# Softmax stage of a four-layer block: in a wide score tile, head 1's products follow head 0's two products behind

## Chip, cores and metric

The kernel runs on one core of a Trainium2 chip. The metric is the device time of one execution in microseconds (us); lower is better. Of the kernel before, three runs are shown, and their median is what a change is measured against.

## What is computed

The reference is a chain of six residual sublayers over x of shape (4, 1024, 128): two top-4-of-32 expert layers around a linear attention, then two top-2-of-8 expert layers around a 16-head softmax attention. Only that attention matters here:

```python
Q = einsum('bmd,hdk->bhmk', x, P_q)          # 16 heads, width 64
K = einsum('bmd,hdk->bhmk', x, P_k)
V = einsum('bmd,hdv->bhmv', x, P_v)
logits = einsum('bhmk,bhnk->bhmn', Q, K) * 8
logits = where(causal, logits, -inf)
w = softmax(logits, axis=-1)                 # 1024 x 1024 per batch and head
o = einsum('bhmm,bhmv->bhmv', w, V)          # the diagonal of w alone
y = einsum('bhmv,hdv->bmd', o, P_o)
```

Since `o` takes the same index twice, only the diagonal of the softmax is needed. For each query that is its own exponential over the sum of the exponentials of its row, so every score has to be formed and summed, but no product of weights and V follows.

## The kernel before, in words

The kernel is written engine by engine: each of its eleven stages gives TensorE, ScalarE, VectorE, GpSimd and SyncE their own list of instructions in a fixed order, and semaphores tie them together. The softmax stage is `softmax_diagonal`. It has 32 units (`UNITS`), one per pair of heads and batch: 8 pairs (`PAIRS`) for each of 4 batches. A head is 64 wide, so the two heads of a pair lie in partitions 0 to 63 and 64 to 127 (`head`), and a score product of one head uses 64 of the 128 rows of the array.

Per unit TensorE does the following (`tensor`, L2858 to L2870):

- It projects queries and keys of the next unit: four banks of three products of 128x512 (`project`, L2807 to L2809). ScalarE copies two of the banks out (L2877) and VectorE the other two (L2883). GpSimd then splits queries and keys into a high and a low part (`split`, L2747 to L2761), since each score is the sum of three products: high x low, low x high, high x high (`passes`).
- It forms the scores of the eight query blocks q of 128 queries. Block q has (q + 1) x 128 keys, its causal part. The order is `ORDER` = 1, 5, 6, 4, 2, 3, 7, and block 0 goes with block 2. Blocks 4 to 7 are wide tiles: `big` (L2819 to L2831) puts each head into two PSUM banks of half the keys each. The others go to `little` (L2841 to L2856), with one bank per head. After tile 1 come the products that give the pair's own scores, eight rows in the trace (`diagonals`, L2837).

In the text "tile 5" is the scores of query block 5, 768 wide, and likewise tiles 6 (896), 4 (640) and 7 (1024). A product of tile 5 has 384 columns, of tiles 6, 4 and 7 448, 320 and 512.

For each tile and head VectorE adds the mask and finds the lowest score, in one custom reduction over the whole tile (L2954, followed by a short read-out row of the accumulator), and ScalarE forms the exponentials in place with that value as bias and sums them (L2934, also followed by a reading of the accumulator). With ScalarE's reading the semaphore `exp_done` rises and the banks are free. Both go through the tiles in the same order, head 0 before head 1.

The eight PSUM banks are given out round robin: a unit takes 4 for the projections and 22 for its tiles, and what takes a bank waits for whoever used it last, eight places before (`wait_bank`, L2724). For the wide tiles that comes to:

- tile 5: head 0 takes the banks of head 1 of the previous unit's tile 7; head 1 takes two projection banks, copied out by VectorE
- tile 6: head 0 takes two projection banks, copied out by ScalarE; head 1 the two banks of tile 1
- tile 4: head 0 takes the banks of tile 5's head 0, head 1 those of tile 5's head 1
- tile 7: head 0 takes the banks of tile 4's head 0, head 1 those of tile 4's head 1

At a batch's end VectorE has some extra work with the sums (`invert`, `divide`, `keep`, `arguments`).

Of the kernel before, what the change touches and what calls it, by code (L numbers as in the profile page):

```python
# [24 lines left out]
P = 128  # L25
# [77 lines left out]
def build(nc, I, out):  # L103
# [9 lines left out]
    def sem(name):  # L113
        if free:
            return free.pop()
        held.append(nc.alloc_semaphore(name))
        return held[-1]
# [58 lines left out]
    def bank(k):  # L176
        return psum[:, k, :]
# [2478 lines left out]
    def softmax_diagonal(split, used):  # L2656
# [5 lines left out]
        S = {n: sem(f"a1_{n}") for n in names}  # L2662
# [14 lines left out]
        ORDER = (1, 5, 6, 4, 2, 3, 7)  # L2677
        LITTLE = {1: (1,), 2: (2, 0), 3: (3,)}
        DIAG, QUARTERS = 1, 4
        NS = 2 * len(ORDER)  # L2680
        BANKS_OF = [4 if q >= BT else 2 for q in ORDER]
        PER_UNIT = NP + sum(BANKS_OF)
# [8 lines left out]
        def first_bank(u, n):  # L2691
            at = before_unit(u) + (NP if u < UNITS - 1 else 0) + sum(BANKS_OF[:n])
            return at % BANKS

        def scored_before(u, n, a):
            return u * NS + 2 * n + a

        def wide(q):
            return (q + 1) * P

        def big_scores(u, n, a):
            k = first_bank(u, n) + 2 * a
            return psum[:, k % BANKS:k % BANKS + 2, 0:wide(ORDER[n]) // 2]

        def small_scores(u, n, q, a):
            at = 3 * P if q == 0 else 0
            return psum[:, (first_bank(u, n) + a) % BANKS, at:at + wide(q)]
# [5 lines left out]
        def spare_of(u, a):  # L2713
            return psum[:, (first_bank(u, ORDER.index(DIAG)) + a) % BANKS, 2 * P:]

        def which(u):
            return u % PAIRS, u // PAIRS

        def turned_own(src):
            return src.rearrange("p (k c e) -> p c k e", k=2, c=QUARTERS)[:, :, :, 0:H1]  # L2720
# [3 lines left out]
        def wait_bank(pe, k, freed, count):  # L2724

            if k in last_user:
                pe.wait_ge(*last_user[k])
            last_user[k] = (S[freed], count)
# [18 lines left out]
        def gpsimd(pool):  # L2747
            def split(v):
                s = v % 2
                wait_out(pool, v, "k")  # L2750
                if v >= 2:
                    pool.wait_ge(S["scored"], (v - 1) * NS)
                pool.tensor_copy(KH[s], KF[s]).then_inc(S["k_hi"], 1)
# [38 lines left out]
        def turn_own(pe, b, dst):  # L2792
            pe.wait_ge(S["diag_in"], (b + 1) * PAIRS)
            for k in range(2):
                last = pe.transpose(dst[:, k * P:(k + 1) * P], own[:, b % 2, k * P:(k + 1) * P], ident[:])
            return last

        def project(pe, v, k):
            kind, half = PROJECT[k]
            g, b = which(v)  # L2800
            wh, wl = (all_w[:, 2 * (kind == "k") + w, g * P:(g + 1) * P] for w in range(2))
            at = slice(b * SEQ + half * BLK, b * SEQ + (half + 1) * BLK)
            to = project_bank(v, k)
            if k == 0 and v < 2:
                pe.wait_ge(split["xl_done"], 2 if v == 0 else 4)
            wait_bank(pe, to, "out_dve" if half else "out_act", out_count(v, kind, half))
            pe.matmul(bank(to), wh, xl[:, at], start=True, stop=False)  # L2807
            pe.matmul(bank(to), wl, xh[:, at], start=False, stop=False)  # L2808
            pe.matmul(bank(to), wh, xh[:, at], start=False, stop=True).then_inc(S["projected"], 1)  # L2809

        def tensor(pe):
            def passes(u):
                s = u % 2
                return ((QH[s], KL[s]), (QL[s], KH[s]), (QH[s], KH[s]))

            def head(w, a, at, n):
                return w[a * DK:(a + 1) * DK, at:at + n]

            def big(u, n):  # L2819
                q = ORDER[n]  # L2820
                half = wide(q) // 2
                for a in range(2):
                    for k in range(2):
                        wait_bank(pe, (first_bank(u, n) + 2 * a + k) % BANKS, "exp_done", scored_before(u, n, a) + 1)
                for p, (qs, ks) in enumerate(passes(u)):
                    for k in range(2):
                        for a in range(2):
                            last = pe.matmul(big_scores(u, n, a)[:, k, :], head(qs, a, q * P, P),  # L2828
                                             head(ks, a, k * half, half), start=(p == 0), stop=(p == 2))
                            if p == 2 and k == 1:  # L2830
                                last.then_inc(S["scored"], 1)  # L2831

            def diagonals(u):
                g, b = which(u)
                pe.wait_ge(S["multiplied"], u + 1)
                for c in range(QUARTERS):
                    last = pe.matmul(spare_of(u, 1)[32 * c:32 * (c + 1), :], pair_ones[:, H1 - 2 * g:3 * H1 - 2 * g],  # L2837
                                     prod[:, c * 2 * P:(c + 1) * 2 * P], start=True, stop=True)
                last.then_inc(S["scored"], 1)

            def little(u, n):  # L2841
                for a in range(2):
                    wait_bank(pe, (first_bank(u, n) + a) % BANKS, "exp_done", scored_before(u, n, a) + 1)
                for q in LITTLE[ORDER[n]]:
                    for p, (qs, ks) in enumerate(passes(u)):
                        for a in range(2):
                            last = pe.matmul(small_scores(u, n, q, a), head(qs, a, q * P, P), head(ks, a, 0, wide(q)),
                                             start=(p == 0), stop=(p == 2))
                            if p == 2 and q == LITTLE[ORDER[n]][-1] and q != DIAG:
                                last.then_inc(S["scored"], 1)  # L2850
                if ORDER[n] == DIAG:
                    g, b = which(u)
                    if g == 0 and b > 0:
                        last = turn_own(pe, b - 1, spare_of(u, 0))
                    last.then_inc(S["scored"], 1)
                    diagonals(u)  # L2856

            for u in range(UNITS):  # L2858
                if 0 < u < UNITS - 1:
                    for k in range(NP):  # L2860
                        project(pe, u + 1, k)
                if u == 0:
                    pe.wait_ge(split["xl_done"], NB)
                pe.wait_ge(S["k_lo"], u + 1)
                pe.wait_ge(S["q_lo"], u + 1)
                for n, q in enumerate(ORDER):
                    if q >= BT:
                        big(u, n)
                    else:
                        little(u, n)  # L2870
            pe.wait_ge(S["exp_done"], UNITS * NS - 2)

# [12 lines left out]
        def batch_of(w, b):  # L2885
            return w[:, b * QT:(b + 1) * QT, :]
# [5 lines left out]
        def invert(dve, b):  # L2892
            dve.wait_ge(S["exp_done"], (b + 1) * PAIRS * NS)
            dve.reciprocal(batch_of(esum, b), batch_of(esum, b)).then_inc(S["inverted"], 1)
# [10 lines left out]
        def arguments(dve, b, src):  # L2905
            all_t = batch_of(arg, b).rearrange("p (c k) e -> p c k e", k=2)
            dve.wait_ge(S["exp_done"], (b + 1) * PAIRS * NS)
            dve.tensor_tensor(all_t, all_t, turned_own(src), ALU.subtract).then_inc(S["arg_set"], 1)
# [3 lines left out]
        def end_pe(pe, j):  # L2912
            if j == 0:
                pe.wait_ge(S["exp_done"], UNITS * NS)
                turn_own(pe, PER - 1, bank(B_OWN)).then_inc(S["own_turned"], 1)
# [85 lines left out]
    def program():  # L3001
# [17 lines left out]
        E2 = dict(E, y_sent=[sem(f"m1e_y_sent{a}") for a in range(2)])  # L3019
        experts_of = moe_experts(E, sort.S)  # L3020
        softmax, unit_first, closing = softmax_diagonal(split, used)
        combine = moe_combine(experts_of.S, split, unit_first)
        sort_2 = sorted_ffn(sort_sems("a1o", False), dn=o_dn, relu=False, ahead=softmax.S, closing=closing, **heads)
# [103 lines left out]
```

## Time and profile before

| | |
|---|---|
| three runs | 1712.15, 1709.97, 1704.38 us |
| median | 1709.97 us |
| profiled execution, from its first to its last instruction | 1712.5 us (the page gives no other time for it) |
| TensorE busy with products | 1436.3 us, 84% of the span |
| VectorE busy | 1339.1 us, 78% |
| ScalarE busy | 1030.1 us, 60% |
| GpSimd busy | 861.2 us, 50% |
| mean granted TensorE clock | 0.938 of full |
| the softmax stage's reductions, L2954 | 512, first at 885.5 us, last at 1353.4 |

All times in the rows are in us from the start of the profiled execution, unless marked ns. PE is TensorE's products, PEld its weight loads, DVE VectorE, ACT ScalarE. A time order gives start, duration, engine, line, operation, and in square brackets how long the engine had been idle before and what ended that. Of instructions that are merged into one row, xN gives their number, and the duration runs from the first one's start to the last one's end.

### The profile page before, as it was taken

Reading aid. Unit: us, or ns where it says so; the run is one execution under the profiler, and the core shown is the slowest. Engines: PE = TensorE matmul, PEld = TensorE weight load, DVE = VectorE, ACT = ScalarE, POOL = GpSimd, SP = SyncE. Lnnn points to the kernel's source line nnn. Section 1 sums busy time; section 2 is a strip of 40 time slices with the busy share of each in tenths; the row PEclk is TensorE's granted clock in tenths of the full one; section 3 lists DMA queues with packets and bytes.
Section 4 is the critical chain, followed back from the end, with each engine's and each line's share of the span. In section 5 each row is a group of like instructions: output and inputs, shape, how many; then the busy total and the mean of one; then the engine's idle time right before and its main releaser. Section 6 shows DMA issues by size and latency. Waiting matters only on the chain.

```text
span 1712.5 us, 30382 instructions
## 1 busy us (share of the span) xinstructions
PE 1436.3 (84%) x8651; PEld 1046.6 (61%) x8653; DVE 1339.1 (78%) x3816; ACT 1030.1 (60%) x2170; POOL 861.2 (50%) x743
## 2 busy tenths in 40 slices
PE   5999999898999995999368878878888799769990
PEld 4778877655666653777245656655656566457770
DVE  7599998566666666787679999999999667857876
ACT  7444442374232316888469988989989622258880
POOL 5756643210133342676656665656656225637663
PEclk9999998999999996999779999999999899879995
DMA  9993010000011104222399900000000001122225
GB/s 189 166 165 44 1 26 26 2 1 13 19 32 42 32 22 98 66 71 66 86 180 166 127 1 1 1 1 1 1 1 1 1 13 35 42 55 68 67 62 148
DMA packets 182172, 91.69 MB, mean 54 GB/s; under 512 B 43829, under 2 KB 176902, under 8 KB 182048
## 3 DMA queue, kind: packets, MB, share of 16 engines
q1 hardware_dynamic: 167840, 71.19, 24.5%
q0 software_dynamic: 9984, 16.89, 3.1%
q10 hardware_dynamic: 4224, 2.10, 0.4%
q8 instruction: 61, 1.00, 0.3%
q14 instruction: 63, 0.52, 0.1%
HBM read 32.59 MB, written 61.18 MB: 55 GB/s over the span
## 4 chain that ended last, share of the span: by engine, by line
PE 63%; DVE 13%; ACT 10%; issue 6%; DMA 4%; POOL 3%; SPq 1%; DVEq 0%; POOLq 0%; ACTq 0%
PE psum L1362 9%; PE psum L2828 7%; ACT psum L2934 7%; PE psum L658 5%; PE psum L659 4%; PE psum L660 4%; DVE psum L2954 4%; PE psum L2807 2%; PE psum L2264 2%; PE psum L2266 2%; PE psum L2265 2%; PE psum L2276 2%; PE psum L2808 2%; PE psum L2809 2%; PE psum L2278 2%
## 5 line engine op out<-in xcount | busy, mean ns | idle before, releaser
L2934 ACT ACTIVATE psum<-psum,gate 128x128 f32<-128x128 f32 (+7 forms) x512 | 366.7, 719 | 51.2 <-DVE gate L2954 44.3
L2954 DVE CUSTOM_DVE_ANT_0 psum<-psum,cmask 128x128 f32<-128x128 f32 (+7 forms) x512 | 375.0, 785 | 28.2 <-PE psum L2828 26.6
L2440 POOL DMA_INDIRECT answers<-ed,answer_to x184 | 201.4, 1094 | 78.7 <-issue 50.2
L1362 PE MATMUL psum<-raw_all,w 128*128 128x512 f32 x384 | 196.3, 594 | 1.5 <-DVE raw_all L1490 1.5
L658 PE MATMUL psum<-xl,wreg 128*128 128x512 f32 x320 | 181.8, 568 | 2.5 <-ACT psum L2934 1.3
L1488 DVE SCALAR_TENSOR_TENSOR raw_all<-psum,hg 128x512 f32<-128x512 f32 x128 | 88.1, 690 | 65.9 <-PE psum L660 64.5
L2828 PE MATMUL psum<-spare_sets_room 64*128 64x384 f32 (+3 forms) x768 | 95.0, 380 | 46.3 <-ACT psum L2934 46.2
L2828 PE MATMUL psum<-hh,hl 64*128 64x384 f32 (+3 forms) x768 | 93.3, 376 | 41.6 <-ACT psum L2934 41.5
L659 PE MATMUL psum<-xh,wreg 128*128 128x512 f32 x320 | 126.6, 396 | 0.0
L660 PE MATMUL psum<-xh,wreg 128*128 128x512 f32 x320 | 126.3, 395 | 0.0
L2828 PEld LDWEIGHTS psum<-spare_sets_room 64*128 64x128 f32 x768 | 71.8, 195 | 71.0 <-ACT psum L2934 59.1
L2356 DVE TENSOR_TENSOR hl<-gate,hh 128x512 fp32r<-128x512 f32 x92 | 63.3, 688 | 63.1 <-ACT hh L2318 32.2
L2828 PEld LDWEIGHTS psum<-hh,hl 64*128 64x128 f32 x768 | 71.0, 194 | 66.7 <-ACT psum L2934 52.4
L1235 POOL TENSOR_TENSOR hl<-hg,hh 128x512 fp32r<-128x512 f32 x65 | 85.8, 1323 | 47.5 <-ACT hh L1167 46.4
L2934 ACT ACTIVATION_READ_ACCUMULATOR psum<-psum,gate 128x1 f32 x512 | 105.1, 205 | 0.0
L819 POOL DMA_INDIRECT rows<-raw_all,row_no x64 | 61.7, 965 | 78.5 <-PE psum L660 63.9
L819 POOL DMA_INDIRECT rows<-row,row_no x64 | 61.9, 966 | 69.1 <-PE psum L660 52.1
L1167 ACT ACTIVATE hh<-hg 128x512 fp32r<-128x512 f32 x86 | 54.1, 632 | 67.1 <-DVE hg L1198 65.2
L201 POOL TENSOR_TENSOR spare_p<-spare_p 128x1 f32<-128x1 f32 x63 | 20.5, 326 | 142.7 <-DVE row_no L780 69.2
L658 PEld LDWEIGHTS psum<-xl,wreg 128*128 128x128 f32 x320 | 61.0, 191 | 39.2 <-issue 27.9
L1362 PEld LDWEIGHTS psum<-raw_all,w 128*128 128x128 f32 x384 | 72.2, 189 | 20.3 <-DVE raw_all L1490 2.3
L2264 PE MATMUL psum<-xl,xh 128*128 128x512 f32 x184 | 81.6, 443 | 0.0
(431 smaller groups left out, 4053.0 us busy)
## 6 DMA issues: line engine op xcount, KB each, us to landing
rows<-blank SPq DMA_DIRECT2D x146, 258.0 KB, 8.3
row<-rows SPq DMA_DIRECT2D x46, 256.0 KB
raw_all<-answers SPq DMA_DIRECT2D x32, 256.0 KB, 4.2
w<-in_L_ffn_W_dram SPq DMA_DIRECT2D x16, 256.0 KB, 3.1
answers<-ed,answer_to POOLq DMA_INDIRECT x184
x<-in_L_attn_x_dram SPq DMA_DIRECT2D x4, 512.0 KB, 6.6
out_dram<-x ACTq DMA_DIRECT2D x8, 256.0 KB, 4.3
rawD<-in_L_ffn_values_dram SPq DMA_DIRECT2D x4, 256.0 KB, 6.5
```

What stands on the lines that cost most here:

```text
L658: pe.matmul(dst, wh, xl[:, blk(i)], start=start, stop=False)
L659: pe.matmul(dst, wl, xh[:, blk(i)], start=False, stop=False)
L660: return pe.matmul(dst, wh, xh[:, blk(i)], start=False, stop=stop)
L819: pool.indirect_dma_start(rows, bass.IndirectOffsetOnAxis(ap=row_no[:, i % 2, c, t:t + 1], axis=0), row_of(i)[:, t, c, :], None).then_inc( ...
L1235: pool.tensor_tensor(hl[:, j % SLOTS, :], kept[n % len(kept)], hh[:, j % SLOTS, :].bitcast(F32), ALU.subtract).then_inc(S["lo_pool"], 1)
L1362: pe.matmul(bank(B_OUT[i % 2]), col(dn, j), hidden[:, n % HID, :], start=(j == 0), stop=(j == nf - 1)).then_inc(S["dn_done"], 1)
L1488: last = dve.scalar_tensor_tensor(out, raw, 0.0, gates_now, ALU.max, ALU.mult)
L2264: pe.matmul(dst, high, xb[:, b.odd, 1], start=True, stop=False)
L2440: pool.indirect_dma_start(answers, bass.IndirectOffsetOnAxis(ap=answer_to[:, out.odd, t:t + 1], axis=0), y_row[:, out.odd, t, :], None, bo ...
L2828: last = pe.matmul(big_scores(u, n, a)[:, k, :], head(qs, a, q * P, P), head(ks, a, k * half, half), start=(p == 0), stop=(p == 2))
L2934: return act.activation(src, src, ACT.Exp, bias=kept_at(arg, u, q, a), scale=-1.0, accum_out=kept_at(esum, u, q, a))
L2954: return dve.tensor_tensor_reduce(src, src, mask, 1.0, 3e38, ALU.add, ALU.min, kept_at(arg, u, q, a))
```

## The change

`big` alone changes. Before, all four bank waits of a wide tile (two banks for each of two heads) stood ahead of its first product, and the twelve products alternated: head 0, head 1, head 0, head 1. Now head 0's six products are counted m = 0 to 5, a bank's wait stands directly ahead of the first product that writes it, and head 1's product m is written after head 0's product m + 2 (`SKEW = 2`). Every product's operands and its bank, the semaphores and the counts waited for are those of before. Head 0's scores are still signalled before head 1's.

```diff
         DIAG, QUARTERS = 1, 4
+        SKEW = 2
...
             def big(u, n):
                 q = ORDER[n]
                 half = wide(q) // 2
-                for a in range(2):
-                    for k in range(2):
+                steps = [(p, k) for p in range(3) for k in range(2)]
+
+                def step(a, m):
+                    p, k = steps[m]
+                    qs, ks = passes(u)[p]
+                    if p == 0:
                         wait_bank(pe, (first_bank(u, n) + 2 * a + k) % BANKS, "exp_done", scored_before(u, n, a) + 1)
-                for p, (qs, ks) in enumerate(passes(u)):
-                    for k in range(2):
-                        for a in range(2):
-                            last = pe.matmul(big_scores(u, n, a)[:, k, :], head(qs, a, q * P, P),
-                                             head(ks, a, k * half, half), start=(p == 0), stop=(p == 2))
-                            if p == 2 and k == 1:
-                                last.then_inc(S["scored"], 1)
+                    last = pe.matmul(big_scores(u, n, a)[:, k, :], head(qs, a, q * P, P),
+                                     head(ks, a, k * half, half), start=(p == 0), stop=(p == 2))
+                    if m == len(steps) - 1:
+                        last.then_inc(S["scored"], 1)
+
+                for m in range(len(steps) + SKEW):
+                    if m < len(steps):
+                        step(0, m)
+                    if m >= SKEW:
+                        step(1, m - SKEW)
```

How TensorE's instructions move is seen in the second unit, tiles 5, 6 and 4. A row is one or several equal matmuls. Semaphores carry the names of their first users: `f0_oT_ready` is `exp_done`, `a0_kv_done` is `out_dve` (VectorE's copies) and `a0_f_done` is `out_act` (ScalarE's copies). Before, on TensorE:

```order
L2828 MATMUL psum<-spare_sets_room 128x384 [waits a0_kv_done,f0_oT_ready]
L2828 MATMUL psum<-spare_sets_room 128x384 x11
L2828 MATMUL psum<-spare_sets_room 128x448 [waits f0_oT_ready,a0_f_done]
L2828 MATMUL psum<-spare_sets_room 128x448 x11
L2828 MATMUL psum<-spare_sets_room 128x320 [waits f0_oT_ready]
L2828 MATMUL psum<-spare_sets_room 128x320 x11
```

And after the change, on TensorE in the same place:

```order
L2830 MATMUL psum<-spare_sets_room 128x384 [waits f0_oT_ready] x2
L2830 MATMUL psum<-spare_sets_room 128x384
L2830 MATMUL psum<-spare_sets_room 128x384 [waits a0_kv_done]
L2830 MATMUL psum<-spare_sets_room 128x384
L2830 MATMUL psum<-spare_sets_room 128x384 [waits a0_kv_done]
L2830 MATMUL psum<-spare_sets_room 128x384 x6
L2830 MATMUL psum<-spare_sets_room 128x320 [waits f0_oT_ready] x2
L2830 MATMUL psum<-spare_sets_room 128x320
L2830 MATMUL psum<-spare_sets_room 128x320 [waits f0_oT_ready]
L2830 MATMUL psum<-spare_sets_room 128x320
L2830 MATMUL psum<-spare_sets_room 128x320 [waits f0_oT_ready]
L2830 MATMUL psum<-spare_sets_room 128x320 x6
```

(Tile 6's rows stand between the two.) The single wait ahead of a tile has become four: two ahead of head 0's first two products, then, behind head 0's third and fourth product, one each ahead of head 1's first two. The other engines have the same instructions in the same order as before.

## Rows read from the trace of the kernel before

**Rows 1.** The page's slices: busy tenths in 40 slices of 42.8 us.

```profile
DVE  7599998566666666787679999999999667857876
ACT  7444442374232316888469988989989622258880
```

**Rows 2.** Busy times by stretch, three of 32 units: PE, PEld, DVE, ACT, POOL, PE clock, DMA.

```profile
943.96:958.90 14.94, 12.71 (x96) 9.93 (x99) 13.45 (x36) 13.17 (x36) 9.11 (x5) 0.89 1.28 171
...
1017.33:1034.45 17.12, 12.99 (x96) 9.42 (x99) 15.66 (x38) 13.30 (x37) 9.08 (x5) 0.90 0.01 1
...
1092.07:1106.26 14.19, 11.57 (x96) 8.48 (x95) 13.46 (x36) 13.15 (x36) 9.13 (x5) 1.00 0.00 1
```

**Rows 3.** Time order of VectorE in the clean unit from 1092.07.

```profile
1093.85 0.97 DVE L2954 CUSTOM_DVE_ANT_0 psum<-psum,cmask 128x768 f32<-128x768 f32 x1 [0.39 <-PE psum L2828]
...
1095.65 0.14 DVE L2954 DVE_READ_ACCUMULATOR2_ANT gate<- 128x1 f32 x1
1095.77 1.10 DVE L2954 CUSTOM_DVE_ANT_0 psum<-psum,cmask 128x896 f32<-128x896 f32 x1
...
1097.84 0.14 DVE L2954 DVE_READ_ACCUMULATOR2_ANT gate<- 128x1 f32 x1
1098.22 0.83 DVE L2954 CUSTOM_DVE_ANT_0 psum<-psum,cmask 128x640 f32<-128x640 f32 x1 [0.24 <-PE psum L2828]
...
1102.57 0.14 DVE L2954 DVE_READ_ACCUMULATOR2_ANT gate<- 128x1 f32 x1
1102.73 1.23 DVE L2954 CUSTOM_DVE_ANT_0 psum<-psum,cmask 128x1024 f32<-128x1024 f32 x1
```

**Rows 4.** Time order of TensorE's products in the same unit.

```profile
1091.38 0.62 PE L2847 MATMUL psum<-hh,hl 64*128 64x256 f32 x6
...
1092.50 1.31 PE L2828 MATMUL psum<-hh,hl 64*128 64x384 f32 x12
1094.28 1.48 PE L2828 MATMUL psum<-hh,hl 64*128 64x448 f32 x12 [0.46 <-ACT psum L2934]
1097.07 1.15 PE L2828 MATMUL psum<-hh,hl 64*128 64x320 f32 x12 [1.31 <-ACT psum L2934]
...
1101.06 1.66 PE L2828 MATMUL psum<-hh,hl 64*128 64x512 f32 x12 [0.85 <-ACT psum L2934]
1102.66 0.50 PE L2807 MATMUL psum<-xl,wreg 128*128 128x512 f32 x1
```

**Rows 5.** Time order of ScalarE in the same unit: tiles 5, 6 and 4.

```profile
1095.71 0.19 ACT L2934 ACTIVATION_READ_ACCUMULATOR psum<-psum,gate 128x1 f32 x1
1095.83 0.88 ACT L2934 ACTIVATE psum<-psum,gate 128x768 f32<-128x768 f32 x1
1096.62 0.19 ACT L2934 ACTIVATION_READ_ACCUMULATOR psum<-psum,gate 128x1 f32 x1
1096.96 0.98 ACT L2934 ACTIVATE psum<-psum,gate 128x896 f32<-128x896 f32 x1
...
1098.91 0.19 ACT L2934 ACTIVATION_READ_ACCUMULATOR psum<-psum,gate 128x1 f32 x1
1099.14 0.77 ACT L2934 ACTIVATE psum<-psum,gate 128x640 f32<-128x640 f32 x1
...
1100.62 0.19 ACT L2934 ACTIVATION_READ_ACCUMULATOR psum<-psum,gate 128x1 f32 x1
```

**Rows 6.** The same order of TensorE, cut off inside tile 5 (stretch 1092.3 to 1092.79).

```profile
1092.50 0.61 PE L2828 MATMUL psum<-hh,hl 64*128 64x384 f32 x4
```

**Rows 7.** Time order of TensorE, start of the projections: product, then next load.

```profile
1088.45 0.50 PE L2807 MATMUL psum<-xl,wreg 128*128 128x512 f32 x1
...
1088.56 0.19 PEld L2808 LDWEIGHTS psum<-xh,wreg 128*128 128x128 f32 x1
```

**Rows 8.** Time order of ScalarE and TensorE after the stage's last exponential.

```profile
1355.79 0.19 ACT L2934 ACTIVATION_READ_ACCUMULATOR psum<-psum,gate 128x1 f32 x1
1356.04 0.69 PE L2795 MATMUL psum<-ident,own 128*128 128x128 f32 x2 [1.50 <-ACT psum L2934]
```

## The prediction

> **What bounds the kernel now.** The slices of the page come first [rows 1]: from the twenty-first slice on, for eleven slices, VectorE and ScalarE are both near nine tenths busy. That is the softmax stage, some 472 of the 1712.5 us, and the only place that the edit touches. Next I cut the stage at the start of each unit (the first score tile of a head pair on VectorE) and asked for the busy times of the 32 stretches [rows 2]. Eighteen units take 14.19 to 14.33 us at full TensorE clock (the row from 1092.07 is one), three take 14.89 to 14.96 with the granted clock at 0.89 (the row from 943.96), eight stand round the ends of batches, where VectorE has extra work (the row from 1017.33 is the longest but one), and the first one and the last two are ramps (15.81, 13.18 and 16.38). In the clean unit TensorE is busy for 11.57, VectorE 13.46, ScalarE 13.15 of 14.19 us: none is full, so a ring of waits sets the length, and the time order shows it.
>
> On VectorE [rows 3] a read-out row normally begins together with the next reduction. Where the reduction is later, VectorE waited: 0.12 us before tile 6 (1095.65 to 1095.77), 0.38 before tile 4 (1097.84 to 1098.22), 0.16 before tile 7 (1102.57 to 1102.73). Tile 5 shows 0.39 as well. TensorE [rows 4] in turn stands 0.46, 1.31 and 0.85 us before tiles 6, 4 and 7, each time for ScalarE's exponentials, which free the banks.
>
> The ring that sets the unit, from one start of tile 5 on VectorE (1093.85) to the next [rows 3 to 5]: ScalarE ends tile 4, head 1, at 1100.62 + 0.19 = 1100.81, so 6.96 us later; TensorE begins tile 7 0.25 after that (1101.06); its six slots last 1.60 until the projections (1102.66); from the first projection to tile 1 it is 2.93 (1088.45 to 1091.38) [rows 4, 7]; and from there to tile 5 on VectorE 2.47 (1091.38 to 1093.85). The sum is 14.21.
>
> **What the change costs and gives.** No instruction is added or removed apart from semaphore waits; 48 products a unit change places, in 32 units.
>
> Slots: two products of different heads start together. The first two pairs of tile 5 take 0.61 us, all six 1.31 [rows 4, 6], so a pair costs (1.31 - 0.61) / 4 = 0.175. In the new order the twelve products need eight slots, if nothing makes head 1 wait: two of head 0 alone, four pairs, two of head 1 alone. A lone product I price as a pair, 0.175, because the nearest row, a product over all 128 rows, also has the next load beside it [rows 7]; it could be no cheaper, and dearer by a whole load, 0.19, which is a rival below. So TensorE may be held 0.35 us longer per tile of this size. In tiles 5 and 6 this lies beside VectorE: head 1 is ready two slots, 0.35, after head 0, and VectorE is busy with head 0 for 0.9. Where head 1's banks come late, in tiles 4 and 7, three products of head 0 run before the wait, and after it six slots remain as before, so nothing is added there; what stands behind that wait are head 0's last three products, and they are released with head 1's first.
>
> The wait itself gets shorter. Today the four bank waits precede the first product, the release at 1096.62 + 0.19 = 1096.81 is followed by the product at 1097.07: 0.26 [rows 4, 5], and 0.25 for tile 7. In the new order head 1's first product has one wait of its own. For one wait the nearest row is the transpose at 1356.04, 0.06 after the release at 1355.79 + 0.19 [rows 8]. I take that and save 0.19; the bounds are 0 and 0.20.
>
> VectorE's waits: tile 6 can start beside tile 5's last product instead of at 1094.28, since its head 0 only needs ScalarE's two copies; tile 5 begins at 1092.50, and with two slots more it has ended by 1092.50 + 1.31 + 0.35 = 1094.16, at least 0.12 before today's start of tile 6, and its last product may run beside tile 6's first: the 0.12 goes. Tile 4, head 0, has three slots of 0.14 fewer behind the release and 0.19 less latency: 0.61 earlier, against a wait of 0.38 and the 0.12 by which VectorE now arrives earlier, so that goes too. Tile 7's 0.16 goes the same way. VectorE alone would then need 14.19 - 0.66 = 13.53 us a unit. Tile 5's own wait stays, since its head 0 follows head 1 of the previous tile 7 and then tile 1's products.
>
> ScalarE is late next. It stood idle 0.22 before tile 6 (a reading starts at 1095.71 and the next exponential at 1095.83, so after the reading at 1096.62 it could be 1096.74; it was 1096.96) and 0.11 before tile 4 (1098.91, so 1099.03, against 1099.14) [rows 5]. Of this some 0.10 remains, since tile 6 still reaches it a little late. It ends tile 4 head 1 about 0.20 earlier than now. The ring becomes (6.96 - 0.20) + (0.25 - 0.19) + 1.60 + 2.93 + 2.47 = **13.82 us**, longer than VectorE's 13.53, so this ring decides and the gain is 0.38 per unit.
>
> Clock: the rows at 0.89 cost 14.94 - 14.21 = 0.73 us each [rows 2]. What TensorE did before the clock fell was to stand still: the longest hole of a clean unit is the 1.31 before tile 4 [rows 4]. Head 0 now fills that hole with three early products, and two lone slots lengthen the tile before it. I expect the three stretches in clean units and two of those beside batch ends to go: 3 x 0.73 + 1.0 = 3.2 us.
>
> Sum: 21 units x 0.38 = 8.0; the eight round batch ends, where VectorE's extra work hides most of it, 8 x 0.2 = 1.6; ramps 0.6; clock 3.2. **13.4 us**. The profiled execution spans 1712.5, which would become 1699.1; that span lies 2.5 above the median of the three runs, 1709.97, from which I forecast 1696.6.
>
> One rule speaks against the edit. The load rows show the next load starting 0.11 after the first projection starts, while that product, over the same rows of the array, runs for another 0.39 [rows 7]. The Trainium skill, page "TensorE: Matmul & The Clock Gate", Part 3, says that a load overlaps running products only when they use another row group. By that rule the projections could not run as they do, so the trace differs from it. Were it true of the lone products, the forecast would be the second rival's.
>
> **Rivals.**
> 1. Larger gain, 0.06: the ring is cut further and VectorE's 13.53 decides. 21 x 0.66 + 5.4 gives about 19 us: 1690.7.
> 2. A lone product also pays for its load, 0.05. Head 0 of tile 5 starts with two of them, in the ring: 2 x 0.19 = 0.38, which takes back the whole 0.38. The clock's 3.2 remains: about 1707. For it: no lone half-array product exists in this trace. Against: the projections.
> 3. The waits moved are not those that end last, 0.13. In tiles 5 and 6 little hangs on banks anyway; if only the shorter latency of tile 7 counts, 21 x 0.19 = 4.0 and half of the clock's: 1704.
> 4. Slower, 0.05: products two steps apart no longer share the array. A tile then takes twelve slots instead of six; tile 5's 1.31 is five slots and 0.43 of start and end, and with the same 0.43 the slots of tiles 6, 4 and 7 come to 0.21, 0.14 and 0.25 [rows 4], so TensorE gets 6 x 0.775 = 4.6 us more a unit. It has 14.19 - 11.57 = 2.6 free [rows 2], the point from which this decides; 2.0 over in 31 units is 62 us: about 1772. Against it: both orders put the two heads side by side in the instruction stream, on other rows and other banks.
> 5. The low clock comes in every unit, 0.03: it is in ten of the 32 units now; 22 more x 0.73 = 16, less the 10.2 otherwise gained: 1716.
>
> **How the numbers follow.** The forecast has 0.68. Its own range is 1690 to 1702: latency saved or not in the ring (21 x 0.19 = 4) and the clock's part absent or complete (3). Half a per cent, 8.5 us, is about what a measurement of this kernel can tell from no change; that line is at 1701.4. Faster: forecast and larger gain, 0.74. Same: the second, third and fifth rival, 0.21. Slower: the fourth, 0.05. The range 1688 to 1706 leaves out the slow cases, the second rival and some noise; the three runs of before alone span 7.8 us.
>
> **What would show it.** Clean units of 13.8 instead of 14.2 us; VectorE's waits before tiles 6, 4 and 7 below 0.05 and the one before tile 5 unchanged; TensorE's tile 4 split, three lone products, a pause, then pairs; the first product after the pause 0.06 behind ScalarE's reading; fewer units with the clock at 0.89. It is wrong if lone products start over 0.25 apart in tile 5, if pairs no longer start together, or if the unit stays at 14.2 with VectorE's waits gone, which would mean that another ring had been as long.

## The result and the profile after

The changed kernel runs in 1691.89 us (median of 4 runs, 1691.54 to 1692.65) against 1708.81 for the kernel before (median of 4, 1704.38 to 1712.15). The recorded ratio is 0.9911, 95% interval 0.9896 to 0.9927 (the two medians alone give 0.9901): faster by 0.9%. The forecast was 1696.6 within 1688 to 1706. One execution in the whole study stands apart, one of ten of e2 with 2832.72 us; it is left out of every comparison, and its cause is not known.

The span of the profiled execution went from 1712.5 to 1690.5 us, 22.0 less. Not all of that is the change's: the softmax stage, from VectorE's first reduction to ScalarE's last reading, went from 470.5 to 453.6 us, 16.9 less. The stage also began 1.1 us earlier and what follows it was 4.0 us shorter, in parts of the program that the edit does not touch. Over all profiles of this study the stage began anywhere from 879.1 to 885.5 us, so differences of a few us are read below from the stage and its units, not from the total.

The page's slices of the changed kernel (busy tenths in 40 slices), TensorE, VectorE and ScalarE:

```profile
PE   5999999898999994999549999999989899769990
...
DVE  7599998567667675787679999999989767857876
ACT  7444432364223234888569999989989622268880
```

Busy times by stretch in the changed kernel (columns as in [rows 2]): a clean unit, a unit with a low clock, and the longest unit.

```profile
1095.15:1108.92 13.77, 12.90 (x93) 9.56 (x92) 13.25 (x35) 12.87 (x36) 9.11 (x5) 1.00 0.01 2
```

```profile
1167.06:1181.52 14.46, 13.61 (x96) 10.85 (x98) 13.42 (x36) 13.05 (x35) 9.14 (x5) 0.88 0.00 1
1237.89:1256.49 18.60, 16.34 (x96) 11.58 (x92) 15.72 (x39) 14.45 (x38) 10.11 (x6) 0.82 0.01 2
```

The clean unit takes 13.77 us where [rows 2] had 14.19. TensorE's busy time went up, from 11.57 to 12.90, though it does the same products: the three early products of a split tile count as busy time alone.

Time order of VectorE in that unit (the reductions of tiles 5, 6, 4 and 7, head 0, with the reading before them), to be held against [rows 3]:

```profile
1096.95 0.97 DVE L2962 CUSTOM_DVE_ANT_0 psum<-psum,cmask 128x768 f32<-128x768 f32 x1 [0.39 <-PE psum L2830]
...
1098.75 0.14 DVE L2962 DVE_READ_ACCUMULATOR2_ANT gate<- 128x1 f32 x1
1098.75 1.13 DVE L2962 CUSTOM_DVE_ANT_0 psum<-psum,cmask 128x896 f32<-128x896 f32 x1
...
1100.85 0.15 DVE L2962 DVE_READ_ACCUMULATOR2_ANT gate<- 128x1 f32 x1
1100.85 0.87 DVE L2962 CUSTOM_DVE_ANT_0 psum<-psum,cmask 128x640 f32<-128x640 f32 x1
...
1105.24 0.14 DVE L2962 DVE_READ_ACCUMULATOR2_ANT gate<- 128x1 f32 x1
1105.24 1.27 DVE L2962 CUSTOM_DVE_ANT_0 psum<-psum,cmask 128x1024 f32<-128x1024 f32 x1
```

Each reduction starts with the reading before it: the waits of 0.12, 0.38 and 0.16 us are gone, and tile 5's 0.39 is unchanged. A new wait of 0.11 stands before tile 1, which starts 0.71 us after the copy before it where 0.60 is usual.

Time order of TensorE in the same unit, against [rows 4], and ScalarE's reading that frees tile 5, head 1:

```profile
1094.49 0.62 PE L2855 MATMUL psum<-spare_sets_room 64*128 64x256 f32 x6
...
1095.61 2.90 PE L2830 MATMUL psum<-spare_sets_room 64*128 64x384 f32 x24
1099.06 0.70 PE L2830 MATMUL psum<-spare_sets_room 64*128 64x320 f32 x3 [0.55 <-ACT psum L2942]
1099.97 1.15 PE L2830 MATMUL psum<-spare_sets_room 64*128 64x320 f32 x9 [0.22 <-ACT psum L2942]
...
1103.04 2.34 PE L2830 MATMUL psum<-spare_sets_room 64*128 64x512 f32 x12
1105.31 0.50 PE L2808 MATMUL psum<-xl,wreg 128*128 128x512 f32 x1
```

```profile
1099.73 0.19 ACT L2942 ACTIVATION_READ_ACCUMULATOR psum<-psum,gate 128x1 f32 x1
```

Tile 4 shows the change as written: three products of head 0, a pause, then nine. The first of the nine starts at 1099.97, 0.05 after the reading ended (1099.73 + 0.19 = 1099.92); before, it was 0.26 [rows 4, 5]. Tile 5 and tile 6 are merged into one row of 24, with no pause.

### The profile page after: what moved, and what is told of

It is laid out like the page before. It is cut to its first block, busy times and chain, and to the rows that moved or that the text cites. A ratio compares the mean times of both kernels' runs of the same rounds, so it can differ in the third digit from the quotient of the medians.

```text
span 1690.5 us, 30128 instructions
## 1 busy us (share of the span) xinstructions
PE 1469.8 (87%) x8653; PEld 1074.6 (64%) x8653; DVE 1335.7 (79%) x3816; ACT 1022.8 (61%) x2170; POOL 861.6 (51%) x743
## 4 chain that ended last, share of the span: by engine, by line
PE 63%; DVE 14%; ACT 8%; issue 6%; DMA 3%; POOL 3%; DVEq 2%; SPq 1%; POOLq 0%; ACTq 0%
PE psum L1362 9%; PE psum L2830 7%; PE psum L658 5%; PE psum L2855 5%; PE psum L659 4%; PE psum L660 4%; ACT psum L2942 4%; DVE psum L2962 3%; PE psum L2808 2%; PE psum L2809 2%; PE psum L2810 2%; PE psum L1121 1%; PE psum L190 1%; PE psum L1123 1%; PE psum L1122 1%
## 5 line engine op out<-in xcount | busy, mean ns | idle before, releaser
L2830 PE MATMUL psum<-spare_sets_room 64*128 64x384 f32 (+3 forms) x768 | 115.3, 369 | 16.2 <-ACT psum L2942 16.2
L2830 PE MATMUL psum<-hh,hl 64*128 64x384 f32 (+3 forms) x768 | 113.1, 376 | 13.4 <-ACT psum L2942 13.4
L2830 PEld LDWEIGHTS psum<-spare_sets_room 64*128 64x128 f32 x768 | 85.9, 185 | 45.3 <-ACT psum L2942 39.3
L2830 PEld LDWEIGHTS psum<-hh,hl 64*128 64x128 f32 x768 | 87.9, 194 | 39.0 <-ACT psum L2942 32.3
L2942 ACT ACTIVATION_READ_ACCUMULATOR psum<-psum,gate 128x1 f32 x512 | 110.2, 215 | 0.0
L659 PEld LDWEIGHTS psum<-xh,wreg 128*128 128x128 f32 x320 | 61.5, 192 | 32.2 <-issue 27.7
```

Of the source, the lines that this page charges most:

```text
L659: pe.matmul(dst, wl, xh[:, blk(i)], start=False, stop=False)
L2942: return act.activation(src, src, ACT.Exp, bias=kept_at(arg, u, q, a), scale=-1.0, accum_out=kept_at(esum, u, q, a))
```

## Experiments

Two theories went into the runs. Theory A is the prediction's: a ring through ScalarE, the bank wait of tile 7, the projections and tile 1 sets the unit. Theory B says that head 0's lead of three products is what gains. The same bookkeeping was also used to choose another tile order, e8, and e9 to e11 test what of that order needs the change.

The results by kernel. Each ratio is to the kernel before, run beside it on the same chip; its median there was 1708.61 us for e1, e2, e6 and e7, 1705.74 for e3, e4, e5 and e8, and 1703.97 for e9 to e12. Stage, clean unit and low clock are read from one profiled execution each. "Stage" is as above, "clean unit" the middle one of those away from the batches' ends at full clock, "low" the number of the first 31 units in which the granted clock fell to half.

```
kernel                      ratio to before  95% interval     stage   clean unit  low
before                                                        470.5   14.22        9
the change                  0.9911           0.9896-0.9927    453.6   13.77        7
e1, lead 0                  0.9890           0.9860-0.9920    453.3   13.77        7
e2, waits ahead             0.9979           0.9961-0.9997    469.2   14.23       10
e3, tile 4 alone            0.9947           0.9930-0.9963    460.8   14.03        4
e4, tile 7 alone            0.9985           0.9966-1.0003    462.9   14.02        8
e5, tiles 5 and 6 alone     1.0019           1.0003-1.0035    470.8   14.22       19
e6, one wait per semaphore  0.9916           0.9891-0.9941    453.3   13.89        3
e7, lead 5                  0.9890           0.9865-0.9914    452.9   13.77        5
e8, new tile order          0.9807           0.9787-0.9828    434.9   13.41        1
e9, that order, old waits   1.0201           1.0177-1.0224    502.2   15.00       14
e10, that order, lead 0     0.9938           0.9919-0.9956    455.5   14.08        2
e11, that order, lead 5     0.9820           0.9803-0.9837    435.1   13.41        1
e12, the change again       0.9925           0.9908-0.9941    456.0   13.77        5
```

### e1: split waits without the lead

```diff
-        SKEW = 2
+        SKEW = 0
```

> SKEW = 0: each bank wait stands ahead of its own first product as in the change, but the heads alternate from the first product on, so head 0 has one product ahead of head 1's wait instead of three. Theory A (the ring through tile 7's wait sets the unit: its length hangs on the time from ScalarE's release to head 1's first product and on ScalarE running without holes): clean units of 13.80, within 0.05 of the change's 13.77, with a wait of 0.1 to 0.2 us before tile 4 on VectorE that ScalarE's backlog covers; more stretches of low clock, since the hole before tile 4 is longer; 1693 to 1698 us. Theory B (the gain is head 0's lead of three products): most of the 0.45 us a unit goes, clean units of 14.1 or more, about 1705 us.

Measured: 1689.66 us, 3 below the range, and clean units of 13.77, as with the change. A clean unit, and VectorE's wait before tile 4 in it:

```profile
1051.44:1065.20 13.76, 12.39 (x96) 8.76 (x97) 13.25 (x36) 12.92 (x35) 9.15 (x5) 1.00 0.01 2
```

```profile
1057.13 0.14 DVE L2962 DVE_READ_ACCUMULATOR2_ANT gate<- 128x1 f32 x1
1057.29 0.83 DVE L2962 CUSTOM_DVE_ANT_0 psum<-psum,cmask 128x640 f32<-128x640 f32 x1
```

The wait of 0.16 us before tile 4 (also the middle value over the clean units) costs nothing, as expected of theory A. Head 0's lead is not what gains in this tile order. That the low clock would come more often was not seen: 7 units here and 7 with the change.

### e2: the changed order with the waits of before

```diff
                 half = wide(q) // 2
+                for a in range(2):
+                    for k in range(2):
+                        wait_bank(pe, (first_bank(u, n) + 2 * a + k) % BANKS, "exp_done", scored_before(u, n, a) + 1)
                 steps = [(p, k) for p in range(3) for k in range(2)]
...
-                    if p == 0:
-                        wait_bank(pe, (first_bank(u, n) + 2 * a + k) % BANKS, "exp_done", scored_before(u, n, a) + 1)
```

> The changed order of products with all four bank waits ahead of a tile's first product, as before the change. Theory A: clean units of 14.22, as before; 1706 to 1711 us. Theory B: head 0 is done three slots earlier relative to the release, so part of the gain stays, 13.9 to 14.0, about 1700 us. Rival of the prediction's slot count: if lone products cost slots (eight instead of six a tile), the 512-column tile 7 ends 0.46 us later and the unit is longer than before, 14.4 or more, about 1716 us; if the two halves of the array run on their own, each tile still spans six slots (1.31 us for tile 5).

Measured: 1704.96 us, 1 below the range, and clean units of 14.23, those of before. The ratio's interval just excludes no change (0.9961 to 0.9997), but the stage is only 1.3 us shorter, inside what the low clock varies. So the order of the products alone brings nothing to the unit. A clean unit of this kernel:

```profile
1040.94:1055.16 14.22, 11.58 (x96) 8.58 (x99) 13.44 (x37) 13.16 (x36) 9.11 (x5) 1.00 0.00 1
```

TensorE's time order in another clean unit, tiles 5, 6 and 4:

```profile
1070.55 1.32 PE L2831 MATMUL psum<-spare_sets_room 64*128 64x384 f32 x12
1072.28 1.49 PE L2831 MATMUL psum<-spare_sets_room 64*128 64x448 f32 x12 [0.41 <-ACT psum L2943]
1075.12 1.15 PE L2831 MATMUL psum<-spare_sets_room 64*128 64x320 f32 x12 [1.34 <-ACT psum L2943]
```

Twelve products in the shifted order take 1.32, 1.49 and 1.15 us, against 1.31, 1.48 and 1.15 in alternation [rows 4]. There are no lone slots: head 1's first product does not wait for head 0's second and third, which are written before it (e7 and the changed kernel show its start). The prediction's eight slots are wrong here.

### e6: one wait per semaphore, order of before

```diff
-                for a in range(2):
-                    for k in range(2):
-                        wait_bank(pe, (first_bank(u, n) + 2 * a + k) % BANKS, "exp_done", scored_before(u, n, a) + 1)
+                needed = {}
+                for a in range(2):
+                    for k in range(2):
+                        at = (first_bank(u, n) + 2 * a + k) % BANKS
+                        if at in last_user:
+                            one, count = last_user[at]
+                            needed[id(one)] = (one, max(count, needed.get(id(one), (one, 0))[1]))
+                        last_user[at] = (S["exp_done"], scored_before(u, n, a) + 1)
+                for one, count in needed.values():
+                    pe.wait_ge(one, count)
```

> The kernel before, with each wide tile waiting once per semaphore, for the highest count alone, instead of four times. Order of products as before. Theory A: the release is followed by the first product after 0.06 instead of 0.25 us at tiles 4 and 7; one such latency per unit lies in the ring, so clean units are 14.0; about 1702 us. Theory B: no head start, no gain, 14.2 us units, 1707 us or more.

Measured: 1693.60 us against the 1702 expected, and clean units of 13.89 against 14.0: a gain of 0.33 of the change's 0.45 us, with every product where it was. A clean unit:

```profile
1050.13:1064.02 13.89, 11.63 (x96) 8.34 (x96) 13.36 (x36) 12.97 (x35) 9.13 (x5) 1.00 0.01 2
```

The time before tile 4, ScalarE's reading and TensorE's first pair:

```profile
1068.56 0.19 ACT L2941 ACTIVATION_READ_ACCUMULATOR psum<-psum,gate 128x1 f32 x1
```

```profile
1068.80 0.41 PE L2835 MATMUL psum<-spare_sets_room 64*128 64x320 f32 x2 [1.07 <-ACT psum L2941]
```

The pair starts 0.05 after the reading's end, where four waits ahead took 0.26 [rows 4, 5]. More than the one latency of tile 7 is gained because ScalarE's hole before tile 4 goes as well. The 0.12 us that e6 lacks lies at tile 6: ScalarE ends that tile's head 0 4.24 us after tile 5's start on VectorE here, and 4.12 after it with the change and with e1 (middle values of the clean units). Head 0 still waits there for head 1's banks, those of tile 1. So of the 0.45 us, 0.33 comes from fewer waits in a row and 0.12 from waits that stand apart by head.

The stage is as short as with the change, 453.3 us, partly because only 3 units here had the low clock. The profiled execution, 1688.43 us, is the fastest of four, 5 us under their median.

### e7: head 1 behind all of head 0

```diff
-        SKEW = 2
+        SKEW = 5
```

> SKEW = 5: head 1's first product comes behind all six of head 0. Theory A: head 1's six slots after its release are still in the ring, so clean units stay at 13.77, within 0.05; perhaps fewer stretches of low clock; 1689 to 1693 us. Theory B: a longer lead gives more, below 13.6. Lone products cost slots: tiles 5 and 6 would span up to eleven slots and the unit would be longer than 14 us; if the halves run on their own, tile 5 still spans six.

Measured: 1689.81 us, clean units 13.77. Nothing is gained or lost by a longer lead. How the two halves of the array run is seen by cutting tile 5 at 0.42 and at 0.72 us after its start (stretches up to 1063.3 and 1063.6):

```profile
1062.88 0.61 PE L2830 MATMUL psum<-spare_sets_room 64*128 64x384 f32 x2
```

```profile
1062.88 0.96 PE L2830 MATMUL psum<-spare_sets_room 64*128 64x384 f32 x5
```

Two products in the first stretch, both head 0's, and head 1 has joined before the second ends: its first product starts 0.46 us after head 0's first, with head 0's third, although all six of head 0's were written ahead of it and three of them had not started. The other units away from the first and the last show the same. The same cut 0.49 us into tile 5 of the changed kernel has six products, three pairs:

```profile
1095.61 0.80 PE L2830 MATMUL psum<-spare_sets_room 64*128 64x384 f32 x6
```

There head 1's first starts 0.01 after head 0's first, past two written ahead of it. In e7 head 1 did not start while four of head 0's products were still waiting, and did with three.

### e3, e4 and e5: the change in some of the tiles

Each takes `big` as changed for the tiles named and as before for the others, by a test on q:

```diff
+                moved = q in (4,)
+                if not moved:
+                    for a in range(2):
+                        for k in range(2):
+                            wait_bank(pe, (first_bank(u, n) + 2 * a + k) % BANKS, "exp_done", scored_before(u, n, a) + 1)
+                lead = SKEW if moved else 0
...
-                    if p == 0:
+                    if p == 0 and moved:
```

with (4,), (7,) or (5, 6).

> The change in tile 4 alone; tiles 5, 6 and 7 have the order and the waits of before. Theory A: VectorE's wait before tile 4 goes, but tile 7's four waits ahead of its first product stay in the ring; clean units of 14.1 to 14.2 and a longer wait before tile 7 (0.38 instead of 0.16); no or few stretches of low clock in clean units; 1702 to 1708 us. Theory B (VectorE's largest wait was before tile 4, so most of the gain is there): 13.9 or less, about 1697 us.

> The change in tile 7 alone. Theory A: one latency of 0.19 leaves the ring, clean units of 14.05 to 14.1, the waits before tiles 6 and 4 stay at 0.12 to 0.18 and 0.3 to 0.38; low clock as often as before; 1702 to 1706 us. With the run of tile 4 alone the two gains are 0.05 to 0.1 and 0.15, and add up to less than the 0.31 or more of both tiles together. Theory B: 14.2, no gain.

> The change in tiles 5 and 6 alone. Theory A: VectorE's 0.12 before tile 6 goes and comes back before tile 4 (0.5 instead of 0.38), the unit stays at 14.22; 1706 to 1711 us. Rival (the head start in every tile counts alike): about 14.1, 1703 us.

Measured: 1696.30, 1701.85 and 1708.40 us, clean units of 14.03, 14.02 and 14.22. A clean unit of the first and of the second, and the whole stage of the third:

```profile
1054.01:1068.05 14.04, 12.32 (x96) 8.91 (x99) 13.33 (x37) 13.04 (x36) 9.13 (x5) 1.00 0.01 2
```

```profile
1038.19:1052.22 14.03, 12.26 (x96) 8.85 (x92) 13.36 (x36) 13.11 (x36) 9.12 (x5) 1.00 0.00 1
```

```profile
882.09:1352.91 470.82, 394.58 (x2919) 303.11 (x2915) 435.49 (x1131) 419.89 (x1087) 282.62 (x155) 0.93 0.21 32
```

Tile 4 alone gained more than expected (0.19 instead of at most 0.12 us a unit, and 6 us below the range of times). Tile 7 alone gained 0.20 a unit, the one latency that was expected, though its whole time is not clear of no change (0.9966 to 1.0003). Tiles 5 and 6 gained nothing; there VectorE's wait moved on to tile 4: 0.47 us in the middle, 0.43 before. The third was 0.2% slower than before. Its low clock goes with that: 19 units where the kernel before had 9, and a granted clock of 0.928 to 0.935 over the ten executions, where 26 of the kernel before on that chip had 0.937 to 0.946. In the profiled executions the two stages are equally long (470.8 and 470.5 us), so that the clock is the whole reason is not shown.

The ring, term by term, decides. The four terms add up to the unit in any kernel; what tells is which of them an edit moves. Middle values over 30 units: from tile 5 on VectorE to ScalarE's end of tile 4, head 1; from there to the projections; to tile 1; to tile 5 on VectorE.

```
kernel                to t4 freed  to projections  to tile 1  to tile 5
before                6.96         1.84            2.95       2.47
the change            6.72         1.64            2.95       2.46
e1, lead 0            6.72         1.64            2.95       2.46
e2, waits ahead       6.96         1.85            2.95       2.47
e3, tile 4 alone      6.77         1.85            2.96       2.47
e4, tile 7 alone      6.96         1.64            2.95       2.47
e5, tiles 5, 6        6.96         1.85            2.95       2.46
e6, fewer waits       6.84         1.64            2.95       2.47
```

Tile 4 moves the first term alone, by 0.19 (ScalarE's hole before that tile, 0.18 us in the middle, is gone); tile 7 the second alone, by 0.20 (the shorter wait); 0.05 is left for tiles 5 and 6 once tile 4 is mended. Theory B falls with e1 and e2.

### e8: another tile order

```diff
-        ORDER = (1, 5, 6, 4, 2, 3, 7)
+        ORDER = (1, 4, 5, 3, 6, 7, 2)
```

> The changed kernel with the tile order 1, 4, 5, 3, 6, 7, 2 (block 0 with 2) instead of 1, 5, 6, 4, 2, 3, 7. With the same durations and waits, in the round robin of the banks, no wide tile then waits for a tile that is less than two places ahead with the projections and tile 1 behind it, and the unit ends with a small tile. By theory A, with every wait worked out from its bank's last user, clean units of 13.4 to 13.5 us, some 9 us less in all: 1680 to 1686. Where it is wrong, the ring is not the one of banks and the unit stays at 13.77 or grows.

Measured: 1670.78 us, ratio 0.9807. Clean units are 13.41, as expected, and the time is 9 us below the range: the stage is 18.7 us shorter than with the change, of which 21 clean units at 0.36 are 7.6, and the rest lies round the batches' ends and in the low clock, which touches one unit instead of 7. VectorE has one wait before a tile left: tile 4's reduction starts 0.40 after the reading before it, where tile 5's started 0.53 after it in the old order. A clean unit:

```profile
1044.29:1057.71 13.42, 13.10 (x96) 9.48 (x92) 13.15 (x37) 13.17 (x37) 9.17 (x5) 1.00 0.01 2
```

### e9, e10 and e11: what of that order needs the change

e9 is the same edit of `ORDER` in the kernel before; e10 and e11 are e8 with `SKEW = 0` and `SKEW = 5`.

> The kernel before with the tile order 1, 4, 5, 3, 6, 7, 2 alone: four bank waits ahead of each wide tile, heads alternating from the start. If the ring of banks is understood, this order is bad with those waits, since tile 5 now takes banks that the tile 4 just before it leaves only late, tile by tile: clean units of 15.2 us (within 0.2), 1 us longer than before, 1735 to 1745 us. If the order is good in itself, whatever the waits, 13.4 to 13.6 and about 1680 us.

> The new tile order with SKEW = 0: waits split by head and bank, but only one product of head 0 ahead of head 1's wait. Head 0's scores then come after head 1's release plus five slots, and in this order that lies in the ring: clean units of 14.1 us (within 0.1), against 13.41 with SKEW = 2; about 1695 us. If the lead plays no part, as in the old order (13.77 with either), 13.41.

> The new tile order with SKEW = 5. Three early products of head 0 are already enough for the ring: clean units of 13.41 as with SKEW = 2, 1669 to 1674 us. If a longer lead still helps, below 13.35.

Measured: 1736.77, 1691.87 and 1671.89 us. One unit of e9 and one of e10:

```profile
1055.09:1070.07 14.98, 11.65 (x100) 8.47 (x92) 13.34 (x36) 13.15 (x36) 9.11 (x5) 1.00 0.00 1
```

```profile
1051.58:1065.66 14.08, 12.63 (x100) 8.63 (x92) 13.39 (x37) 13.16 (x36) 9.18 (x5) 1.00 0.01 2
```

With the old waits the order is 2% slower than the kernel before; split waits take 0.92 us off each unit, the lead another 0.67, and a longer lead nothing. So the lead, which did nothing in the old tile order, is worth 0.67 us a unit where neighbouring wide tiles pass banks to each other directly. The units measured 15.00, 14.08 and 13.41 where 15.2, 14.1 and 13.41 were worked out (the last is e8's value carried over), and e8's own 13.4 to 13.5 was worked out before any run had this order. That is the strongest support for the ring of banks. e10's time, 1691.87, came 3 us below the 1695 expected.

### e12: the change once more

> The changed kernel itself, unaltered, beside the others on one chip: clean units of 13.77, 1687 to 1693 us, so that its distance to the new tile order (18 to 21 us) and to the kernel before can be read on the same chip.

Measured: 1690.00 us, 0.9925 (0.9908 to 0.9941), clean units 13.77. On this chip the new order with SKEW = 5 is 18 us below it.

## Why the prediction was right

**The ring.** Its four terms were put at 6.76, 1.66, 2.93 and 2.47, 13.82 us in all; the trace has 6.72, 1.64, 2.95 and 2.46, 13.77. The two reasons given for the first two terms were shown apart by e3 and e4. The clean units' gain was put at 0.38 and was 0.45. Of the difference 0.03 is that 14.19 was taken as the unit of before where 14.22 is the middle; the rest is in the ring, most of it the first term. ScalarE's hole before tile 4 was put at 0.11 from one unit and is 0.18 in the middle of the clean ones, and the hole before tile 6, from which 0.12 was hoped for, gave only 0.05.

**The wait.** From ScalarE's release to the first product took 0.26 and now takes 0.05, forecast 0.06; e6 shows it without the reordering. What the change's words describe, head 1 two products behind, is not what shortened these units: e1 has the gain without it and e2 has it without the gain.

**The slots.** This step failed, at no cost. "In the new order the twelve products need eight slots" held nowhere that banks were free: e2's tiles span 1.32, 1.49 and 1.15 us, six slots. The second and fourth rival fall with it: tile 4's three lone products take 0.70 us in all, and nothing was lost to loads. In e7 the third lone product of tile 5 starts 0.17 us after the second, the distance of pairs, and the load of the second starts 0.11 us after the first product has begun. The rule on loads in Part 3 of the Trainium skill's page "TensorE: Matmul & The Clock Gate" would have put a load between them, and the trace differs from it. Of the other rivals, the first was not reached (13.77 and not 13.53), the third falls with e3, and the fifth with 7 low units, 5 in e12.

**VectorE.** The waits went before tiles 6, 4 and 7 and stayed before tile 5, as forecast. Not forecast was a wait of 0.11 us before tile 1, which gives a part back on VectorE, but tile 1 lies on the ring and the ring's terms came out as forecast.

**The sum.** The stage is 16.9 us shorter, the forecast was 13.4. The forecast time is 4.7 us too high: 3.5 from this, and 1.2 because the median of before is 1708.81 with the fourth run and was 1709.97 with three. That the medians lie 16.9 apart like the two stages is chance: the profiled spans lie 22.0 apart. The 21 units between the batches' ends gave 9.9 (8.0 and 2.2 of clock were forecast for them), the eight around the ends 3.3 (1.6, and 1.0 of clock), and the ramps 3.7 where 0.6 stood. That the 9.9 stands so near 10.2 is in part luck: 21 x 0.45 is 9.5, so the clock gave these units 0.4 and not 2.2, and the larger gain of the ring made up for it. The ramps are the term that was mis-sized most; the last unit alone gave 2.0 us. Before, VectorE waited long there ahead of tiles 5 and 6:

```profile
1342.88 0.97 DVE L2954 CUSTOM_DVE_ANT_0 psum<-psum,cmask 128x768 f32<-128x768 f32 x1 [1.06 <-PE psum L2828]
...
1345.47 1.10 DVE L2954 CUSTOM_DVE_ANT_0 psum<-psum,cmask 128x896 f32<-128x896 f32 x1 [0.65 <-PE psum L2828]
```

In the changed kernel the same two start 0.14 and 0.10 us after the reading before them:

```profile
1325.86 0.97 DVE L2962 CUSTOM_DVE_ANT_0 psum<-psum,cmask 128x768 f32<-128x768 f32 x1
...
1327.76 1.10 DVE L2962 CUSTOM_DVE_ANT_0 psum<-psum,cmask 128x896 f32<-128x896 f32 x1
```

Part of it is the low clock that the unit had before. In e2, which has the waits of before, the last unit ran at the full clock and took 14.44 us, against 15.36 before and 13.34 in the changed kernel. By that some 0.9 us is the clock's and 1.1 the waits', an estimate from one execution each.

**The clock.** Five stretches were to go. The count in the first 31 units fell only from 9 to 7, and one unit of 18.60 us with two of them end to end (mean clock 0.82) gave back 2.9. This step failed: filling the hole before tile 4 was to end them. What moves this count is not settled: it was 3 with e6, 19 with e5, 5 and 7 in two profiles of the changed kernel. TensorE's longest pause in a clean unit goes with it in part: 1.65 us in e5 (19 units), 1.49 in e9 (14), 1.35 in e2 (10), 1.34 before (9), 1.26 in e4 (8), and 0.15 in e8 (1). But e6 has 1.09 with 3 units, and the change 0.55 with 7. That fits a clock that falls after TensorE has stood still only loosely, and no run varied the pause alone.

## What to carry to other kernels

Write a chain of engines that hand buffers round as a ring, with the time of each hand-over from the trace, and look which term an edit shortens: here it gave the unit of eleven other kernels to within about 0.2 us, one of them 2% slower and two 2% faster (e9 was the farthest off, 15.2 for 15.0). Before reordering work, look at how many waits stand between a release and the first instruction that needs it; waiting once for the highest count of a semaphore took 0.20 us off the hand-overs of tiles 4 and 7 and needed no other change. Tile 6, which waits for two semaphores, kept its 0.14. A reordering that brings nothing in one order of the tiles can be what makes a better order possible, so try them together.

## What the runs showed of the hardware that was not expected

- Products over the lower and the upper 64 rows of the array are not bound to their written order. With free banks, head 1's first product started 0.01 us after head 0's first, past two others of head 0 (the change), and in e7 past three of six. Where head 1's product had to wait for a semaphore, head 0's products behind it stood still too: in tile 4 of the changed kernel three ran and the fourth came with head 1's first.
- Four semaphore waits ahead of one product, of which the last ends it, cost 0.25 to 0.26 us from the release to the product; a single wait 0.05 to 0.06. What counts is how many separate semaphore instructions run behind the release: two before tile 4 in the kernel before (at 1096.85 and 1096.97, the load at 1097.04), none in e6. Before tile 6 it is one in both kernels, though four waits are written in the first and two in e6, and both take 0.14.
- A lone product in one half of the array costs the same 0.17 us (384 columns) as a pair, and no less.
